# Routing, shared FFN and experts of a mixture-of-experts layer put in one stage with one written order

## The reference

```
scores = softmax(xn @ gate_w.T)                 # 16 experts
topk_w, topk_i = top_k(scores, 4); topk_w /= sum(topk_w)
# each expert takes its first CAP = 128 tokens, by rank in token order
xg    = xpad[buf]                               # 16 x 128 rows gathered
mid   = silu(xg @ w_gate) * (xg @ w_up)         # 256 -> 176, per expert
eout  = mid @ w_down * weight
y[buf] += eout                                  # scattered back
shared = silu(xn @ sw_gate) * (xn @ sw_up) @ sw_down   # 352 wide
ffn   = y + shared
```

## Time and profile before

| | |
|---|---|
| median of 3 runs | 2451.95 us (2450.97 to 2452.54) |
| the profiled execution | 2449.4 us |
| its span, first to last instruction | 2447.6 us |
| mean granted clock of PE | 0.934 |
| busy, PE / DVE / ACT / POOL | 2073.9 / 1646.4 / 1413.6 / 887.4 us |
| first routed layer | 0 to 222.2 us |
| second routed layer | 364.1 to 578.9 us |

### The profile page before, as it was taken

How to read it: one execution, slowest core, us unless ns; L and a number is a source line. 1 busy time by engine, 2 the same in 40 slices (tenths; PEclk the granted TensorE clock), 3 DMA queues, 4 the chain that set the end, 5 groups by cost and what they waited for, 6 DMA issues and landing times. The chain is left out here.

```text
span 2447.6 us, 42392 instructions
## 1 busy us (share of the span) xinstructions
PE 2073.9 (85%) x14632; PEld 1862.0 (76%) x14632; DVE 1646.4 (67%) x3777; ACT 1413.6 (58%) x3646; POOL 887.4 (36%) x746
## 2 busy tenths in 40 slices
PE   4953886872977999999999999999999999999688
PEld 3842784761867888888888888888888888888668
DVE  6465766475347777777777777777777777777643
ACT  3342553342335776766766767667667677676532
POOL 1463001564223343343343343433433434324232
PEclk9975897975988999999999999999999999999989
DMA  4064002063000000000000000000000000000100
GB/s 138 1 182 96 1 8 95 30 178 98 1 33 3 10 3 8 10 3 8 10 3 5 4 12 5 3 12 5 4 10 8 4 10 4 7 1 1 40 9 26
DMA packets 43986, 66.81 MB, mean 27 GB/s; under 512 B 5632, under 2 KB 29440, under 8 KB 43648
## 3 DMA queue, kind: packets, MB, share of 16 engines
q1 hardware_dynamic: 37632, 55.71, 7.0%
q0 software_dynamic: 6144, 8.39, 2.0%
HBM read 48.89 MB, written 15.20 MB: 26 GB/s over the span
## 5 line engine op out<-in xcount | busy, mean ns | idle before, releaser
L1003 ACT ACTIVATE phase_pt_hi<-phase_ring 128x512 fp32r<-128x512 f32 (+3 forms) x680 | 345.7, 536 | 205.3 <-PE phase_ring L988 201.9
L963 ACT ACTIVATE phase_p<-phase_scores,phase_bias 128x512 f32<-128x512 f32 (+3 forms) x680 | 416.5, 625 | 74.0 <-DVE phase_bias L951 72.4
L1008 DVE TENSOR_TENSOR phase_pt_lo<-phase_ring,phase_pt_hi 128x512 fp32r<-128x512 f32 (+3 forms) x680 | 394.7, 603 | 76.3 <-ACT phase_pt_hi L1003 76.2
L944 DVE TENSOR_REDUCE phase_peaks<-phase_scores 128x1 f32<-128x512 f32 (+3 forms) x680 | 396.2, 603 | 55.6 <-PE phase_scores L936 27.1
L988 PE MATMUL phase_ring<-sb_ident,phase_p 128*128 128x128 f32 x2312 | 348.0, 275 | 39.0 <-DVE phase_pt_lo L1008 30.3
L115 PE MATMUL phase_y<-phase_pt_hi,phase_v_hi 128*128 128x256 f32 x1152 | 333.3, 289 | 0.0
L988 PEld LDWEIGHTS phase_ring<-sb_ident,phase_p 128*128 128x128 f32 x2312 | 263.0, 141 | 81.8 <-issue 47.7
L117 PE MATMUL phase_y<-phase_pt_hi,phase_v_lo 128*128 128x256 f32 x1152 | 322.1, 280 | 0.0
L116 PE MATMUL phase_y<-phase_pt_lo,phase_v_hi 128*128 128x256 f32 x1152 | 321.6, 279 | 0.0
L1749 POOL TENSOR_TENSOR phase_straight<-phase_rot,phase_rope 64x512 f32<-64x512 f32 x128 | 163.6, 1278 | 373.5 <-ACT phase_rot L1628 373.5
L933 PE MATMUL phase_scores<-phase_k_hi,phase_q_hi 128*128 128x512 f32 (+2 forms) x640 | 253.6, 396 | 9.9 <-POOL phase_k_lo L1758 5.4
(11 more groups left out here) (271 smaller groups left out, 5480.6 us busy)
## 6 DMA issues: line engine op xcount, KB each, us to landing
phase_raw_up<-expert_up SPq DMA_DIRECT2D x32, 352.0 KB, 3.1
phase_raw_dn<-expert_down SPq DMA_DIRECT2D x32, 256.0 KB, 2.7
y_rows<-phase_zero SPq DMA_DIRECT2D x8, 512.0 KB, 7.8
xn_rows<-phase_ln_xn SPq DMA_DIRECT2D x8, 512.0 KB, 3.2
phase_ln_xn<-y_rows SPq DMA_DIRECT2D x8, 512.0 KB, 5.5
phase_raw_qk<-qk SPq DMA_DIRECT2D x16, 256.0 KB, 2.6
phase_raw_up<-up SPq DMA_DIRECT2D x4, 704.0 KB, 6.7
sb_x<-x SPq DMA_DIRECT2D x4, 512.0 KB, 5.6
```

Of the source, the lines that this page charges most:

```text
L944: dve.tensor_reduce(self.peaks[:, t % 2, c:c + 1], self.scores[:, at:at + self.width(t, c)], AX.X, ALU.max).then_inc(*self.peaked.one)
L963: act.activation(self.p[:, at:at + width], self.scores[:, at:at + width], ACT.Exp, bias=self.bias[:, t % 2:t % 2 + 1], accum_out=self.sums ...
L1003: act.activation(hi, value, ACT.Copy).then_inc(*self.t_hi.one)
L1008: dve.tensor_tensor(lo, value, as_f32(hi), ALU.subtract).then_inc(*self.t_lo.one)
```

## The change

`Route`, `Routes` and `Experts` become one class, `Routed`, and after the norm all queues follow one list of steps, `plan_order`.

- The norm's halves are separated: PE makes the logits of chunks 0 and 1 before it turns the second half. The shared FFN's weights are split inside the norm (`dve_weights`).
- `dve_choose` works on the logits instead of the softmax. Exp is taken later, and the routing weights are made (`dve_weigh_tokens`) after the first marks. They are written to DRAM in 16 columns behind each row of `xn_rows`, so that a gather brings a token's weights with it, and DVE scales by `x_rows[.., H + n]`.
- Slots are found for two experts at once: `info` has three numbers per token and is the stationary operand, and `hot` of two experts, 256 columns, moves. Two small transposes bring the result back, and three DVE operations make the row numbers of both.
- Experts' matmuls take plain float32 tiles, with no split. Rows have four buffers, weights four, loaded four experts ahead; the first four at the stage's start.
- The shared FFN's second product is multiplied by DVE straight from PSUM, and all splits are on DVE; the sums are added to `x` by DVE from PSUM in one operation of 512 columns. Gate, up and sums have one PSUM bank each.
- POOL has only memsets and the two indirect DMAs.

```diff
+    def plan_order(self):
+        shared = []
+        for q in range(NCH * ISM):
+            shared.append([("gate", q)] + ([("round", q - 1)] if q else []))
+            shared.append([("up", q)])
+            if q % ISM == 0 and q:
+                shared += [[("sums", q // ISM - 1, half)] for half in range(2)]
+        shared += [[("round", NCH * ISM - 1), ("sums", NCH - 1, 0)], [("sums", NCH - 1, 1)]]
+        ...
+        fill(2)
+        order.append(("rank",))
+        fill(2)
+        order += [("mark", 0), ("mark", 1)]
+        fill(1)
+        order += [("find", 0), ("weights",), ("mark", 2), ("mark", 3)]
+        fill(2)
+        order += [("found", 0), ("fetch", 0), ("fetch", 1), ("find", 1)]
+        fill(2)
+        order += [("found", 1), ("fetch", 2), ("fetch", 3), ("mark", 4), ("mark", 5)]
+        fill(2)
+        order.append(("x", 0))
+        fill(1)
+        order.append(("feed", 0))
+        spread = len(shared) / (NE + 1)
+        given = 0.0
+        for n in range(NE):
+            p = n // 2 + 2
+            if n + 1 < NE:
+                order.append(("x", n + 1))
+            given += spread / 2
+            fill(int(given))
+            given -= int(given)
+            order.append(("h", n))
+            if n % 2 == 0 and p < NE // 2:
+                order.append(("find", p))
+            if n + 1 < NE:
+                order.append(("feed", n + 1))
+            if 2 * p + 2 + n % 2 < NE:
+                order.append(("mark", 2 * p + 2 + n % 2))
+            if n % 2 == 0 and p < NE // 2:
+                order.append(("found", p))
+            order.append(("down", n))
+            if n + 4 < NE:
+                order.append(("fetch", n + 4))
+            order.append(("place", n))
+            given += spread / 2
+            fill(int(given))
+            given -= int(given)
+        fill(len(shared))
+    # SP, after the loads, zeros and normalized rows
+        sp.wait_ge(*self.weighted[tag])
+        sp.dma_start(core.xn_rows[0:T, H:H + NE].rearrange("(t p) e -> p t e", p=P), self.weight[:]).then_inc(*self.weights_out.one)
+        for n in range(self.SLOTS, NE):
+            sp.wait_ge(*self.e_downed[tag, n - self.SLOTS])
+            self.sp_expert(sp, n)
+    # PE
+            elif what == "sums":
+                pe.wait_ge(*self.left[tag, c * ISM + ISM - 1])
+                if c or half:
+                    pe.wait_ge(*self.added[tag, c - 1 + half, 1 - half])
+            ...
+            elif what == "find":
+                pe.wait_ge(*self.marked[tag, 2 * g + 1])
+                ...
+                for t in range(NT):
+                    done = pe.matmul(self.find_ps, self.info[:, t, :], self.hot[:, 2 * g % 4:2 * g % 4 + 2, :, t], start=t == 0, stop=t == NT - 1)
+            elif what == "feed":
+                ...
+                for k in range(HK):
+                    done = pe.matmul(self.gu_ps, self.x_cols[:, n % 2, k * P:(k + 1) * P], self.e_up[:, n % self.SLOTS, k, :],
+                                     start=k == 0, stop=k == HK - 1)
+            elif what == "h":
+                pe.wait_ge(*self.e_multiplied[tag, n])
+                if n:
+                    pe.wait_ge(*self.weighed[tag, n - 1])
+    # ACT, ahead of the order
+        act.wait_ge(*self.shifted[tag])
+        act.activation(self.score[:], self.score[:], ACT.Exp).then_inc(*self.powers.one)
+    # DVE
+            elif what == "down":
+                dve.wait_ge(*self.e_downed[tag, n])
+                if n >= 2:
+                    dve.wait_ge(*self.placed[tag, n - 2])
+                dve.tensor_scalar(self.out[:, n % 2, :], self.down_ps, self.x_rows[:, n % 4, H + n:H + n + 1], None, ALU.mult).then_inc(*self.weighed.one)
+    # POOL
+            if what == "fetch":
+                if n == 0:
+                    pool.wait_ge(*self.zeros_out[tag, NCH + 1])
+                    pool.wait_ge(*self.norm.rows_out[tag, NCH - 1])
+                    pool.wait_ge(*self.weights_out[tag])
+                pool.wait_ge(*self.got[tag, n // 2])
+                if n >= 4:
+                    pool.wait_ge(*self.weighed[tag, n - 4])
+                pool.indirect_dma_start(self.x_rows[:, n % 4], None, core.xn_rows, ...)
+            elif what == "place":
+                pool.wait_ge(*self.weighed[tag, n])
+                if n:
+                    pool.wait_ge(*self.placed[tag, n - 1])
+                pool.indirect_dma_start(core.y_rows, ..., self.out[:, n % 2, :], None, compute_op=ALU.add).then_inc(*self.placed.one)
```

More of the change, by code:

```diff
@@ L304, in __init__ @@
+        self.info = sb("info", [P, NT, 3], BF16)
         self.logits_t = sb("logits_t", [NE, T])
-        self.score, self.sel, self.eq, self.a, self.b = (sb(n, [P, NT, NE]) for n in ("score", "sel", "eq", "a", "b"))
-        self.rank, self.rank_b = sb("rank_all", [P, NT, NE]), sb("rank_b", [P, NE, NT], BF16)
+        self.score, self.over, self.chosen = (sb(n, [P, NT, NE]) for n in ("score", "over", "chosen"))
+        self.tied = [sb(f"tied{n}", [P, NT, 8 + NE]) for n in range(2)]
         self.best = sb("best", [P, NT, 8])
@@ L318, in __init__ @@
         self.raw_up, self.raw_dn = sb("raw_up", [P, HK, n_up]), sb("raw_dn", [P, ISM, H])
[L319 to L324, removed]
@@ new lines, in __init__ @@
+        self.out = sb("out", [P, 2, H])
+        self.norm = Norm(core, sb, tag, self.turn_banks, keep_rows=True, first=start is not None)
+        sig = lambda what: core.flag("routed_" + what)
+        self.order = self.plan_order()
+        of = lambda what: [(tag, *step[1:]) for step in self.order if step[0] == what]
+        experts, one = [(tag, n) for n in range(NE)], [tag]
+        self.gate_in, self.consts_in = core.loads("routed_in_gate"), core.loads("routed_in_consts")
+        self.gate_in.plan(one)
@@ new lines, in __init__, with fill @@
+        self.placed = core.loads("expert_placed")
+        for s in (self.x_turned, self.x_copied, self.fed, self.e_gated, self.e_multiplied, self.h_turned, self.h_copied,
+                  self.e_downed, self.weighed, self.placed):
+            s.plan(experts)
+    def plan_order(self):
[6 more added lines that the diff above has]
+        shared += [[("round", NCH * ISM - 1), ("sums", NCH - 1, 0)], [("sums", NCH - 1, 1)]]
+        order = []
+        def fill(count):
+            for _ in range(min(count, len(shared))):
+                order.extend(shared.pop(0))
+        fill(2)
[38 more added lines that the diff above has]
+        fill(len(shared))
+        return order
@@ L410, in pe @@
             self.start.pe(pe)
-        self.norm.pe_turn(pe)
-        pe.wait_ge(*self.gate_lo[tag])
-        pe.wait_ge(*self.norm.ready)
-        for c in range(NCH):
-            where = slice(c * CH, (c + 1) * CH)
-            products(pe, self.down_ps[0:NE, c, :], [self.w_hi[:, k, :] for k in range(HK)], [self.w_lo[:, k, :] for k in range(HK)],
-                     [(core.xt_hi[:, k, where], core.xt_lo[:, k, where]) for k in range(HK)]).then_inc(*self.logits.one)
-        pe.wait_ge(*self.logits_out[tag, NCH - 1])
@@ L471, in act, with pe_up @@
+    def pe_up(self, pe, bank, q, n):
+        core, (c, m) = self.core, divmod(q, ISM)
+        where, at = slice(c * CH, (c + 1) * CH), (2 * m + n) * P
+        return products(pe, bank, [self.up_hi[:, k, at:at + P] for k in range(HK)], [self.up_lo[:, k, at:at + P] for k in range(HK)],
+                        [(core.xt_hi[:, k, where], core.xt_lo[:, k, where]) for k in range(HK)])
     def act(self, act):
```

807 lines of the change are left out of this document (348 added, 459 removed).

## The result

The changed kernel takes 2461.2 us (median of 6 runs, 2455.6 to 2462.1), the kernel before 2451.8 us (6 runs): ratio 1.0037, 95% interval 1.0024 to 1.005, so about 9 us slower where 103 us less were forecast. The profiled execution took 2462.1 us, its span is 2460.3 us, its clock 0.935.

The account below looks back on a forecast made before the run. Bounds: DVE's chain, then PE, then rings through PE, ACT, DVE and POOL's scatters in the two routed stages. Savings of 51 and 52 us make 103, giving 2349 us on the median; range 2330 to 2372 us.

Parts of the forecast that it names:

- term 2: First routed stage, from mask to first scatter-add: 39.9 us in all, with finds at 1.9 us each.
- slower: Whole kernel slower than before, if plain float32 matmuls average beyond 1.41 us; chance 0.03.
- The rival of a lower clock: PE work in each routed stage stays at clock 0.76, taking 33 us more per stage: 2415 us; chance 0.06.
- a feed of over 2 us: Sign of being wrong: an expert's feed on PE, forecast at 1.27 us, takes over 2 us.
- dear float32: Experts' float32 matmuls with open weight loads, up to 1.32 us: 2439 us; chance 0.06 still gaining, 0.03 slower.
- Until the mask: Start of first routed stage: choosing on logits makes the mask ready at about 42.3 us instead of 51.55.
- Mask to first scatter-add: First routed stage: 27.4 us of PE work plus waits, 39.9 us in all; first scatter-add at 82.2 us.
- Plain float32: Experts' matmuls: four passes, 0.64 us at 352 columns and 0.47 at 256; feed 1.27, down 0.95.
- Scatter 0 to 15: First routed stage: PE's 76.8 us, 5.1 per expert, plus stalls make 81.7; last scatter-add starts at 163.9 us.
- The end: Last scatter-add to the next stage's load: 7.2 us as before, load issued at 171.1 instead of 222.2 us.
- Layers: Both routed stages: first ends at 171.1 us instead of 222.2, second takes 163.0 us instead of 214.8.
- Scatters set the pace: Rival between scatter 0 and 15: near-one-pass float32 leaves scatters at 66.3 us binding, 2312 us; chance 0.11.

Follow-up runs that it names:

- two tiles inside: Changed kernel with the marks laid out with two token tiles innermost, so moving elements lie 4 bytes apart; 2344.2 us, ratio 0.955 to the kernel before.
- The probes: Eight groups of 16 extra matmuls at varied spacing behind the fourth pair's find, added to the kernel with marks as stationary operand; 2417.0 us in one run.
- one-pass version: Kernel with marks as stationary operand, experts' feed and down products reading only the upper 16 bits in one bf16 pass; 2332.3 us, ratio 0.951.
- four tiles inside: Changed kernel with the marks laid out with four token tiles innermost, so moving elements lie 8 bytes apart; 2368.1 us, ratio 0.965 to the kernel before.

## Why the prediction was wrong

The step that failed is in term 2: "Its moving operand is bf16 with 32 bytes between elements. The trace has that stride only as a weight load ... at that pace a find costs 2.1. I take 1.9." It costs 7.45. The upper bound came from a row of the other path into PE: loading weights at that spacing takes 66 ns per 128 columns, moving columns 233. With the 16 finds that is 16 x 5.55 = 89 us, and with it goes a clock of 0.74 to 0.83: 16 us more of PE's time in each layer, of which some 13 show (the layers are 57.0 and 57.8 us longer than with two tiles inside, 44.4 of them by the finds). 2349 + 89 + 26 = 2464, against 2461 measured; this is no test, since the 26 are read from the same times. No rival priced the moving operand's spacing, and all of "slower" had a chance of 0.03. The rival of a lower clock was named with a wrong cause (gaps of PE): PE had none to speak of. One sign of being wrong did come, a feed of over 2 us (2.71), but by the half clock behind a find and not by dear float32.

A rule bears on this that the prediction left out: the Trainium skill, SBUF — State Buffer, section Door 1: The DMA port swizzle, in its note on cachelines, says SBUF is read in lines of 16 bytes and that at least two accesses must fall in a line for full pace, so that 8 bf16 elements of stride are free. The probes agree that spacing costs, but not where it begins: 8 bytes, two elements in a line, already cost double (0.226), and of the spacings tried 4 bytes was the widest that cost next to nothing (0.113 against 0.109).

By the prediction's steps, in the changed kernel and, in brackets, with two tiles inside:

- *Until the mask*: ready at 40.8 [40.2], forecast 42.3; rank_b at 45.4, forecast near 45. Right.
- *Mask to first scatter-add*: 101.7 [79.3], forecast 82.2. Three finds account for 16.7 of the 19.5 us. The routing weights, given 2 of 0 to 4.5 us, cost none: issued at 53.97, landed after 3.0 us, and the first gather waited for its row numbers. The price of 85 ns per short packet was far too high: 128 on each engine, landing included, took 3.0 us. (Fourteen slices of 0.1125 us are 1.6 us, not 1.4, so the stretch itself gave 96 ns.) (The Trainium skill, DMA: Bandwidth & Descriptors, opening table, has transfers under 512 bytes read, modify and write; what part of the 3.0 us that is, no run here shows.)
- *Plain float32*: forecast 0.64 and 0.47 us per matmul, measured 0.59 and 0.435 at full clock (121.30 to 122.48 and on to 123.35, by two). Right in kind, 8% high.
- *Scatter 0 to 15*: 119.1 us [84.3], forecast 81.7. Five finds give 28 us. They leave 6.5 of the 34.8 us between the two kernels, by the clock: the same matmuls run at 0.83 in the one and at 1.00 in the other. With two tiles inside the sum is near (84.3), but one sign fails: POOL was to wait for DVE and not for the landing, and nine of its sixteen scatters wait for a landing, 24.7 us in all. PE's order and the scatters' chain set this stretch together.
- *The end*: 6.8 us [7.0], forecast 7.2. Right.
- *Layers*: 227.5 and 218.5 us [170.5 and 160.7], forecast 171.1 and 163.0.
- *Scatters set the pace* had chance 0.11 at 4.42 us each. Their pace beside gathers and loads is 4.9 in the one-pass version, so PE's 5.1 led by less than was thought, and even in one pass the time was 2332, not 2312.

So 103 us were there to be had (2344 to 2351 us were measured), in the main by the mechanism that was forecast: PE full between marks and scatters, at clock 1.00 from 60 to 160 us with two tiles inside. That these times meet 2349 so closely is in part luck, since the 2 us for the late weights were not needed and the scatters took 2.6 more. One operand's layout took all of it.

## What to carry to other kernels

Price a strided operand by a row of the same path: a weight load's pace says nothing of a moving operand's. Where the elements of a moving bf16 operand would lie 8 bytes or more apart, put two of the inner index side by side: here this left DVE's compare at 1.22 us and gave PE its full pace, while a fully contiguous layout made the compare 2.28. A busy PE is no proof of progress: read the mean time of each form of matmul and the clock beside the busy share.

## What the runs showed of the hardware that was not expected

- With 3 stationary columns, 256 moving bf16 columns took 0.109, 0.113, 0.226, 0.451 and 0.467 us at 2, 4, 8, 16 and 32 bytes between elements; with 128 stationary columns 0.460 at 32 bytes.
- The granted clock fell from 1.00 to 0.50 with PE busy all the time, in a row of 16 matmuls at 0.451 us (99 to 105 us of the probes) and in finds at 0.465; with finds at 0.226 us per matmul (four tiles inside) it stayed at 1.00 from 80 to 160 us.
- With the marks as stationary operand (three moving columns per weight load) it was 0.88 from 60 to 80 us, against 1.00 with two tiles inside. The kernel before, with six moving columns per weight load, held 0.99, so the form alone need not be the reason.
- 2048 runs of 64 bytes were written to DRAM and had landed 3.0 us after their issue.
